# A four-layer attention and feed-forward kernel: order of the last transposes, filler matmuls and width of two routing matmuls

## What is computed

```python
x = x + _L0_xattn_ref(ctx_1024, _layernorm(x))        # alignment by dynamic time warping
x = x + _L0_ffn_ref(_layernorm(x), ...)               # quantised feed-forward with a convolution
x = x + _L1_xattn_ref(ctx_1024, _layernorm(x), ctx_1024, ...)   # attention, 8 heads
x = x + _L1_ffn_ref(_layernorm(x), ...)               # 8 experts, the best 2 of each token
x = x + _L2_xattn_ref(_layernorm(x), ctx_1024, ctx_1024, mask, ...)  # attention, 16 heads
x = x + _L2_ffn_ref(_layernorm(x), ...)               # soft mixture of 64 experts
x = x + _L3_xattn_ref(_layernorm(x), ctx_1024, ctx_1024, ...)   # attention, 16 heads
x = x + _L3_ffn_ref(_layernorm(x), ...)               # 6 experts, best 2 by an anchor code
```

## Time and profile before

| what | value |
|---|---|
| median of 3 runs | 1062.32 us (1062.26 to 1062.55) |
| profiled execution, its own time | 1062.32 us |
| span of that execution | 1060.5 us |
| mean granted PE clock | 0.934 |
| PE busy | 851.3 us (80%) |
| DVE busy | 790.3 us (75%) |
| ACT busy | 570.1 us (54%) |
| POOL busy | 445.8 us (42%) |

### The profile page before, as it was taken

One profiled execution on the slowest core, in us unless ns is written; L12 is line 12 of the kernel. 1 busy time (PEld: TensorE's weight loads), 2 busy tenths in 40 slices (PEclk: granted clock), 3 DMA queues, 4 the chain that ended last, 5 costly groups with the idle time before them and its releaser, 6 DMA issues. The chain is left out here.

```text
span 1060.5 us, 26265 instructions
## 1 busy us (share of the span) xinstructions
PE 851.3 (80%) x10319; PEld 613.3 (58%) x10319; DVE 790.3 (75%) x1840; ACT 570.1 (54%) x1300; POOL 445.8 (42%) x286
## 2 busy tenths in 40 slices
PE   4173499689739995789868999989898989887888
PEld 3062354678526764344546767767676767654557
DVE  4989786678765544788787859595868777789974
ACT  4172144466614444467687464656557474347774
POOL 4101030498226775298206434343525262708820
PEclk9597699899959998699989999999999999999999
DMA  5421000400061114000100000000000000000001
GB/s 156 110 58 80 1 1 0 157 11 2 12 222 46 54 51 100 13 1 2 32 20 2 27 3 26 3 27 2 27 3 27 27 2 2 2 2 2 1 2 40
DMA packets 27127, 35.94 MB, mean 34 GB/s; under 512 B 7836, under 2 KB 20445, under 8 KB 26239
## 3 DMA queue, kind: packets, MB, share of 16 engines
q1 hardware_dynamic: 21310, 27.84, 8.2%
q0 software_dynamic: 2496, 5.12, 1.7%
q10 hardware_dynamic: 3200, 1.31, 0.5%
HBM read 26.98 MB, written 7.27 MB: 32 GB/s over the span
## 5 line engine op out<-in xcount | busy, mean ns | idle before, releaser
L1833 PE MATMUL soft_expert_ps<-soft_W,soft_slots 128*32 128x128 f32 x4096 | 137.8, 277 | 14.8 <-issue 8.6
L2104 DVE TENSOR_TENSOR soft_outs<-soft_expert_ps,soft_bias 128x512 f32<-128x512 f32 x128 | 87.2, 687 | 76.1 <-PE soft_expert_ps L1833 76.1
L1833 PEld LDWEIGHTS soft_expert_ps<-soft_W,soft_slots 128*32 128x32 f32 x4096 | 106.1, 110 | 47.3 <-issue 43.5
L1925 ACT ACTIVATE soft_slots<-soft_slot_ps 128x512 f32<-128x512 f32 x128 | 69.4, 593 | 80.0 <-PE soft_slot_ps L1819 78.3
L945 POOL TENSOR_TENSOR l_prob<-l_prob,l_inv 128x1024 f32<-128x1024 f32 x48 | 91.3, 1902 | 40.5 <-DVE l_inv L1099 39.4
L2006 POOL TENSOR_TENSOR l_ring<-l_ring,soft_inv 128x1024 f32<-128x1024 f32 x15 | 39.0, 2628 | 105.9 <-DVE soft_inv L2097 57.7
L1084 DVE TENSOR_REDUCE l_under<-l_score 128x16 f32<-128x1024 f32 x48 | 58.7, 1223 | 27.3 <-PE l_score L1165 14.8
L2006 POOL TENSOR_TENSOR soft_spread<-soft_spread,soft_inv 128x1024 f32<-128x1024 f32 x16 | 41.3, 2614 | 73.9 <-DVE soft_inv L2097 73.9
L1847 PE MATMUL soft_mix_ps<-soft_outs,soft_combT 128*64 128x128 f32 x1024 | 70.0, 279 | 1.5 <-DVE soft_acc L2120 1.5
L974 PE MATMUL l_turned<-ident,l_prob 128*128 128x128 f32 x384 | 52.4, 280 | 22.7 <-POOL l_prob L945 22.7
L1048 ACT ACTIVATE l_probT<-l_turned 128x512 f32<-128x512 f32 x96 | 52.1, 594 | 33.1 <-PE l_turned L974 33.1
(11 more groups left out here) (435 smaller groups left out, 2174.9 us busy)
## 6 DMA issues: line engine op xcount, KB each, us to landing
moe_w<-in_moe_W SPq DMA_DIRECT2D x2, 2048.0 KB, 10.1
soft_W<-in_soft_W SPq DMA_DIRECT2D x16, 256.0 KB, 2.8
kept<-early SPq DMA_DIRECT2D x1, 2048.0 KB, 6.3
l_keys<-in_moe_b SPq DMA_DIRECT2D x1, 2048.0 KB, 9.1
l_asked<-kept SPq DMA_DIRECT2D x1, 2048.0 KB, 13.8
ctxT<-in_ctxT SPq DMA_DIRECT2D x1, 1024.0 KB, 5.1
moe_rows<-xn_tok SPq DMA_DIRECT2D x4, 256.0 KB, 3.7
expert_rings<-moe_back SPq DMA_DIRECT2D x4, 256.0 KB, 5.8
```

The lines of the kernel that those rows point to most:

```text
L1833: last = nc.tensor.matmul(expert_ps[c][32 * j:32 * j + 32, h, tt, :], slots[u % 3][:, h, tt, 128 * c + 32 * j:128 * c + 32 * j + 32], W[i ...
L1925: last = nc.scalar.activation(slots[u % 3][:, h], slot_ps[h][:], ACT.Copy)
L2104: nc.vector.tensor_tensor(outs[u % 3][:, c].rearrange("p h t d -> p (h t) d"), expert_ps[c][:].rearrange("p h t d -> p (h t) d"), bias[i % ...
```

## The change

Five edits, with nothing else altered:

1. In `attend`, PE's transposes of group 3 are issued before the reading of group 2, not of group 3. The wait for the last addition and the 12 filler matmuls ahead of them now stand in every attention, not in L2 alone, and 8 fillers follow them.
2. In `attend`, DVE always normalises group 3 before it copies group 2; before, it did so in L2 alone.
3. `route_group` and `code_group` multiply by the matrix itself, 8 and 6 columns.
4. At the end of `moe`, the queries of group 0 are asked after the transposes of group 2, and 10 fillers come ahead of those transposes and 10 ahead of the transposes of group 3.
5. At the end of `soft_moe`, the queries of group 0 are asked after the transposes of group 2.

```diff
--- before.py
+++ after.py
@@ -1012,11 +1012,11 @@
             norm.turn(pe, 1)
             norm.turn(pe, 2)
             for g in range(G):
-                if g == 3:
-                    if not read:
-                        pe.wait_ge(added, T)
-                        keep_busy(nc, core, spare, 12)
+                if g == 2:
+                    pe.wait_ge(added, T)
+                    keep_busy(nc, core, spare, 12)
                     norm.turn(pe, 3)
+                    keep_busy(nc, core, spare, 8)
                 if read:
                     norm.ready(pe, g)
                     read(pe, g, mix).then_inc(read_done, 1)
@@ -1136,11 +1136,8 @@
             dve.wait_ge(added, T)
             norm.statistics(T - 1)
             norm.variances(dve, 3)
-            if read:
-                norm.take_v(dve, 2)
             norm.normalise(dve, 3)
-            if not read:
-                norm.take_v(dve, 2)
+            norm.take_v(dve, 2)
             norm.take_v(dve, 3)
             if on_dve:
                 dve.wait_ge(read_done, G)
@@ -1174,12 +1171,10 @@
         return nc.tensor.matmul(out[:, 0:128], core.ones16[:], core.bias16[:, 0, :], start=False, stop=True)
 
     def route_group(pe, g, bank):
-
         if g == 0:
             pe.wait_ge(core.loaded["gate"], 32)
         for t in range(4 * g, 4 * g + 4):
-            last = nc.tensor.matmul(bank[:, 8 * t:8 * t + 128], core.xnT[:, 128 * t:128 * t + 128],
-                                    core.Wg[:].unsqueeze(1).broadcast_to([128, 16, 8]), start=True, stop=True)
+            last = nc.tensor.matmul(bank[:, 8 * t:8 * t + 8], core.xnT[:, 128 * t:128 * t + 128], core.Wg[:], start=True, stop=True)
         return last
 
     def take_gates(dve, bank):
@@ -1441,11 +1436,13 @@
             norm.turn(pe, 0)
             keep_busy(nc, core, spare, 10)
             norm.turn(pe, 1)
+            pe.wait_ge(hiddenT_done, TILES)
+            keep_busy(nc, core, spare, 10)
+            norm.turn(pe, 2)
             pe.wait_ge(takenT_done, TILES)
             queries.ask(pe, 0)
-            pe.wait_ge(hiddenT_done, TILES)
-            norm.turn(pe, 2)
             queries.ask(pe, 1)
+            keep_busy(nc, core, spare, 10)
             norm.turn(pe, 3)
             queries.ask(pe, 2)
             queries.ask(pe, 3)
@@ -1689,8 +1686,7 @@
         if g == 0:
             pe.wait_ge(core.loaded["code"], core.code_loads)
         for t in range(4 * g, 4 * g + 4):
-            last = nc.tensor.matmul(bank[:, E * t:E * t + 20 * E], core.xnT[:, 128 * t:128 * t + 128],
-                                    core.code_w[:].unsqueeze(1).broadcast_to([128, 20, E]), start=True, stop=True)
+            last = nc.tensor.matmul(bank[:, E * t:E * t + E], core.xnT[:, 128 * t:128 * t + 128], core.code_w[:], start=True, stop=True)
         return last
 
     def take_codes(act, bank):
```

## The result

The changed kernel takes 1068.68 us (median of 6 runs, 1065.95 to 1069.88) against 1062.29 for the kernel before: ratio 1.0063, 95% interval 1.0051 to 1.0077. It is 6.4 us slower, where I had forecast +1.2 and a range that ended at 1065.6. The profiled execution is one of the longer ones: 1070.25 us, span 1068.5, mean granted clock 0.923 (before 0.934). So the differences of the stages in it add up to 7.9 us and not to 6.4.

What follows compares the result with a forecast made beforehand. PE was taken as the bound: its order at L1 attention's end, gapless half-clock work at the first mixture's end. -0.1 + 1.4 + 0 + 0 - 0.1 = +1.2 on 1062.3 gave 1063.5 us; 8 in 10 between 1060.7 and 1065.6.

Steps and rivals of the forecast that it cites:

- Narrow passes, time of one: Routing passes in the attention tails: 8 columns start 0.11 us apart, bound by weight loading, so narrowing saves nothing.
- Sum of the attention tails, -0.1 each: Ends of L1 and L3 attention: earlier copy offset by fillers and the postponed group, -0.1 us each.
- rival B: Last stage: idle room from narrow reads at L3's end lowers its clock, costing 1.7 us; kernel 1065.2; chance 0.20.
- A: L1 and L3 attention tails: narrow passes cheap, 0.065 us or less, -1.4 us each; kernel 1060.9; chance 0.13.
- C: First mixture's end: clock rises earlier, -1.1 us in place of +1.4; kernel 1061.0; chance 0.15.
- First mixture, +1.4: End of the first mixture: asks and fillers at half clock delay group 3's transposes; +1.4 us, bounds -1.1 and +3.1.
- Soft mixture's tail, 0: End of the soft mixture: the moved ask fits between transposes; 0, at worst 0.2 us, while the clock is full.
- Shift of the soft mixture's rounds, 0 with 0.9 either way: Soft mixture: an upstream shift may add or remove clock falls of 0.88 us; 0 in the sum, +-0.9 in range.
- L2 attention, 0: End of L2 attention: the copy of group 3 covers the 8 added fillers; 0 us, 0.3 without that cover.

Runs made afterwards that it cites:

- e7: The whole change with routing matmuls of 64 and 60 columns in place of 8 and 6, against the kernel before: 1081.48 us, ratio 1.0029.
- e2: The kernel before with only the routing matmuls narrowed to 8 and 6 columns: 1083.62 us, ratio 1.0049 against the kernel before.
- e13: The whole change with one 128-column bf16 filler ahead of every narrow routing matmul, against the kernel before: 1083.31 us, ratio 1.0045.
- e15: The kernel before with only the soft mixture's ask for group 0 moved behind the transposes of group 2: 1082.52 us, ratio 1.0029.
- e10: The kernel before with four repeated DVE bias additions at the first mixture's end, against the kernel before: 1088.87 us, ratio 1.0080.
- e18: The kernel before, unchanged, run once more for its profile: traced execution 1082.4 us, the 17 runs beside it 1075.2 to 1083.7.
- e17: e10 plus 60 fillers on PE behind its last ask in the first mixture, against the kernel before: 1082.05 us, ratio 1.0026.

## Why the prediction was wrong

**Narrow passes, time of one.** Right: the first sixteen (1.86 us) start 0.11 apart, as their weight loads do and as the 128-column passes of before did, so nothing was saved. At half clock the same sixteen take 3.52, and they and their loads start 0.21 apart: the load slows with the clock as the pass does. The rule of the Trainium skill that I weighed (TensorE: Matmul & The Clock Gate, section LDWEIGHTS (loading the stationary operand)), 0.107 us for 128 columns, agrees at full clock only.

**Sum of the attention tails, -0.1 each.** The step that failed. It took 0.11 us for all sixteen last passes, that is the full clock to the end. The L1 stage came out 2.3 us longer: 3.52 in place of 1.76 for the passes, and 1.71 us for the transposes and 8 fillers ahead of them (286.58 to 288.29), where I had 0.89. L3 attention is 3.8 us longer: e7, which has its early fall but not the one in the tail, takes 81.32 us, so about 1.8 belong to the early fall and 2.0 to the tail. I had seen in rival B that narrow reads let the clock fall, but set the fall behind the stage, where the last stage would pay, and gave it 0.20; that the tails themselves would run at half clock in both attentions wasn't in any case.

**Rivals A and C.** A is wrong, narrow passes aren't cheap. C, an earlier rise in the mixture's tail, seems to come about in part in the two traces of the result: the rise stands 3.4 us behind the start of group 2's transposes, 5.9 before. But over all traces it is 3.4 to 5.8 us with the ask moved and 3.6 to 6.0 with it in its old place, so edit 4 doesn't bring the rise forward. Its first fillers end early, and PE then idles for 1.64 us ahead of these transposes (0.69 before).

**Rival B.** That narrow reads lower the clock for the last stage is what happened. Its price, 1.7 us, was low: the last stage is 2.6 us longer since its low stretch lasts 5.2 us, to 1040.9. The reason I gave for it was wrong in part: I spoke of idle room, yet PE is busy for 3.38 of 3.40 us ahead of e2's fall at 284.5, and in the changed kernel it works without a gap ahead of the fall at 286.6 (1.80 of 1.80 us). e7 and e13 show that what is streamed decides.

**First mixture, +1.4.** Right in mechanism: the ask and the fillers go at half clock. The tail is 0.2 us longer in the two traces of the result, which is luck of where the clock rose (443.6, with the work without a gap begun at 440.2 only), and about 1.3 in the mean of all traces. Mis-sized was what follows, which I had at 0: edit 4 alone costs 4.7.

**Soft mixture's tail, 0.** Right in the changed kernel's trace (6.50 us, as before), wrong where the clock falls: 1.0 to 1.2 us in three of seven traces, and e15 loses 3.2 us in all. I named the case inside rival B at +1.0, which is its price in the tail, and left it out of the sum.

**Shift of the soft mixture's rounds, 0 with 0.9 either way.** The size of one fall holds: the rounds of the changed kernel are 49.65 us, or 50.52 with a fall, and the stage has fewer long ones, which gives back 1.67 us. The range was too narrow since such falls stand in every stage, not in that one alone: in the changed kernel L3 attention has one more from 959.0 to 965.8, which with its tail makes the 3.77 us. That this fall comes from the change isn't shown; e10 and e18 have one at about that place without edit 5.

**L2 attention, 0.** Right: 81.02 and 81.02.

## What to carry to other kernels

A PE that the profile shows as fully busy lost its clock here when its passes streamed 8 columns between weight loads, and kept it with 64. Before narrowing an operand, see whether the pass is bound by its weight load, for then the columns are free (0.11 us a pass with 8, 64 or 128) and may be what keeps the clock up. Work that fills a hole ahead of PE-bound work can be worth its place: with an ask taken out of one hole three of seven traces have a fall in that tail, and six fillers put into another brought its tail from 6.7 to 7.8 us down to 5.5. An order edit must be priced with the granted clock of every stretch it touches and of the stage behind it, and its error is some microseconds, not tenths, where that clock is near a change.

## What was not expected of the hardware

- Narrow fp32 passes, each with a weight load of 128 columns, start 0.11 us apart at full clock and 0.21 at half clock.
- With the same 29 matmuls and the same busy share, the clock fell behind passes of 8 columns (e2) and held behind those of 128 (e18).
- PE idle for 4.24 us ahead of a stage cost 4.7 us in it, over three falls (e10: 85.73 against 81.03 in e17, with the same shift).
- The five edits, each measured alone, sum to 12.3 us and together cost 8.8. That they share falls of the clock, or avoid them for one another, is a guess; the difference is hardly clear of the intervals.
- In the experiments, on five chips, the first mixture takes 15 to 19 us longer in every kernel (20 in e10, shift included) than in the two traces of the result; nothing that was run explains it.
